# A GNN-and-mixture kernel for Trainium2: each group of TensorE products in the edge stages is announced by a drain behind it instead of by its last product

## The chip, the cores and the metric

The kernel runs on one core of one Trainium2 chip. The metric is device time of one execution in microseconds (us), the median of several runs without the profiler. Before the change it is 1890.13 us (three runs, 1889.97 to 1891.54).

## What is computed

Two layers over a graph of N = 3125 nodes with D = 256 features and E = 50000 edges (src, dst), the edges sorted by dst. Cut to what matters here:

```python
xn = layernorm(x)
# layer 0: attention over the edges (1 head, with self loops), then an LSTM cell; plus a linear-attention mixture
e     = leaky_relu(a_src[src] + a_dst[dst])
alpha = segment_softmax(e, dst)
agg   = segment_sum(alpha[:, None] * xp[src], dst)      # edge sums
x = x + cell(tanh(agg + bias)) + mixture0(xn)
x = x + top2_experts0(layernorm(x))
# layer 1: the same with 8 heads, no self loops, elu; plus a gated linear-attention mixture
x = x + elu(edge_sums(xn)) + mixture1(xn)
x = x + top2_experts1(layernorm(x))
```

dst is drawn as 3125 u^2 with u uniform, so the low-numbered nodes have by far the most edges.

## The kernel before, in words

Nodes are held in 25 tiles of 125 (`P`, `NT`). The sorted edges are cut into 98 blocks (`NBLK`) of 512, each of 4 parts of 128 (`BW`). A block that holds edges of several tiles is visited once for each, which makes 122 steps (`STEPS` = 98 + 25 - 1) in each layer. `edge_sums` (from L589, called once a layer) runs these steps on all engines at once, with the order of each engine's work written out by hand and semaphores between the engines:

- **POOL** (L671 to L680) issues 4 indirect gathers for each block, one for 128 edges, into a ring of `R` = 8 blocks (`rows`). From the ninth block on it waits for `freed`.
- **SP** (L657 to L668) waits for the landing of each block, tells `landed`, and passes `freed` on after the sums of an older block (`summed` in layer 0, `weighed` in layer 1).
- **DVE** (L836 to L855), in step i: reduces the scores (L832), marks which edge belongs to which node (`mark`, L812), makes the logits (L842 to L848), adds finished sums to `acc` (`add`, L805), does its part of the mixture, and weighs (`weigh`, L819 in layer 0, L822 in layer 1).
- **ACT** takes exponentials (L745 to L752) and copies the turned marks out of PSUM (`keep`, L762, after a wait for `turned` and `scored`).
- **TensorE** (PE), in step i: `sums(i - 4)` (L699: 4 f32 products, each of which the profile records as 2), `scores(i - 2)` (L707: 4 small bf16 products), the mixture's products `side.tensor(pe, i)`, then `turn(i)` (L718: 4 bf16 products). The last product of each group carries the semaphore increment that the waiting engines need (`summed`, `scored`, `turned`).

The mixtures `Mix0` and `Mix1` hang on the steps as `side`. In Mix0, a tile's keys (L1717) and its key-value sums (L1705, L1706) fall due in 5 of 9 steps from step 4 to about step 50; a tile's hidden layer (L1770) in each step from 71 to 95; its output (L1761) in each step from 89 to 113. In Mix1, keys (L1997) are due in steps 2 to 26, the context (L2015, then L2004 two steps later) in steps 31 to 59, and in every second step from 67 to about 117 an output product (L2047) and a query (L2052, L2056). The same form of announcement stands behind each of them.

The form that the change touches, and the loop that orders TensorE's work:

```python
ins = pe.matmul(sum_banks[p % 2][0:P, 0:W], left, right, start=(w == 0), stop=(w == BW - 1))
ins.then_inc(summed, 1)
...
for i in range(STEPS + 4):
    if valid(i - 4):
        sums(i - 4)
    if valid(i - 2):
        scores(i - 2)
    side.tensor(pe, i)
    if valid(i):
        turn(i)
```

Of the kernel before, what the change touches and what calls it, by code (L numbers as in the profile page):

```python
# [588 lines left out]
def edge_sums(nc, m, tag, H, side_of=None):  # L589
# [8 lines left out]
    with Stage(nc) as c:  # L598
# [58 lines left out]
        with nc.Block() as block:  # L657
# [24 lines left out]
            @block.tensor  # L682
            def _(pe):
                bounds.tensor(pe)
                slot_of = column(pe, SLOT, R - 1)

                def sums(p):
                    slot = slot_of(p) if H == 1 else None
                    pe.wait_ge(weighed, p + 1)
                    if H > 1:  # L690
                        pe.wait_ge(laid, p + 1)
                    if p >= 2:
                        pe.wait_ge(added, p - 1)
                    for w in range(BW):
                        if H == 1:
                            left, right = won[:, p % 2, w, :], rows[:, bass.ds(slot, 1), w, :].rearrange("p a x -> p (a x)")
                        else:
                            left, right = one[:, p % O, w, :], msg[:, p % 2, w, :]
                        ins = pe.matmul(sum_banks[p % 2][0:P, 0:W], left, right, start=(w == 0), stop=(w == BW - 1))  # L699
                    ins.then_inc(summed, 1)  # L700

                def scores(p):
                    pe.wait_ge(kept, p + 1)
                    if p >= 1:
                        pe.wait_ge(zchain, 4 * p - 3)
                    for w in range(BW):
                        ins = pe.matmul(scores_of[p % 2][:, w, :], oneT[:, p % 2, w * 128:(w + 1) * 128],  # L707
                                        stage[:, p % 4, :], start=True, stop=True)
                    ins.then_inc(scored, 1)

                def turn(p):
                    pe.wait_ge(marked, p + 1)
                    if p >= 1:
                        pe.wait_ge(kept, p)
                    for w in range(BW):
                        at = turn_bank[0:P, w * 128:(w + 1) * 128]
                        flags = one[:, p % O, w, :] if H == 1 else upper(one[:, p % O, w, :])
                        ins = pe.matmul(at, flags, ident[:, :], start=True, stop=True)  # L718
                    ins.then_inc(turned, 1)

                for i in range(STEPS + 4):
                    if valid(i - 4):
# [6 lines that stand above are left out]
# [905 lines left out]
class Mix0:  # L1634
# [59 lines left out]
    def tensor(self, pe, i):  # L1694
# [6 lines left out]
        for t in self.scale(i, 1):  # L1701
            s = t % self.KV
            pe.wait_ge(self.normed, t + 1)
            for k in range(KD):
                pe.matmul(total[:, k * W:(k + 1) * W], kv[0:P, s, k, 0:128], kv[0:P, s, 2 + k, :], start=False, stop=False, skip_group_check=True)  # L1705
                ins = pe.matmul(total[:, 2 * W + k:2 * W + k + 1], kv[0:P, s, 2 + k, 0:128], kv[0:P, s, 0, 128:129],  # L1706
                                start=False, stop=False, skip_group_check=True)
            ins.then_inc(self.summed, 1)
        for t in self.key(i):
            if t == 0:  # L1710
                pe.wait_ge(self.centred, 3)
            if t == 1:
                pe.wait_ge(self.qkept, 1)
            if t >= 2:
                pe.wait_ge(self.biased, t - 1)
            for k in range(KD):
                ins = pe.matmul(m.bank[4 + 3 * (t % 2)][0:P, :], m.xT[:, k, tile_cols(t)], m.wkv[:, k, :], start=(k == 0), stop=(k == KD - 1))  # L1717
            ins.then_inc(self.made, 1)
        if i == self.CLOSE:
            pe.matmul(total[:, 0:260], self.zeros[:, 0:128], self.zeros[:, :].unsqueeze(1).to_broadcast([P, 2, 130]),  # L1720
                      start=False, stop=True).then_inc(self.summed, 1)
        if i == self.CLOSE + 2:
            pe.wait_ge(self.widened, 1)
            for k in range(KD):
                ins = pe.matmul(m.bank[7][:, k * 128:(k + 1) * 128], self.wide[:, k, :], m.ident[:, :], start=True, stop=True)
            ins.then_inc(self.spread, 1)
        if i == 2:
            pe.wait_ge(self.split, 1)
            for k in range(KD):
                for b in range(KD):  # L1730
                    at = k * D + b * 128
                    ins = pe.transpose(m.bank[7][:, at:at + 128], m.wq[:, b, k * 128:(k + 1) * 128], m.ident[:, :])
            ins.then_inc(self.qturned, 1)
        if i == self.FOLD:
            pe.wait_ge(self.mixer, 1)
            for k in range(KD):
                ins = pe.transpose(m.bank[7][:, k * 128:(k + 1) * 128], m.kv[:, k, :], m.ident[:, :])
            ins.then_inc(self.flipped, 1)
        if i == self.FOLD + 2:
            pe.wait_ge(self.biased, NT)  # L1740
            pe.wait_ge(self.flat, 1)
            for k in range(KD):
                ins = pe.matmul(m.bank[4][:, k * D:(k + 1) * D], self.kvT[:, k, :], m.w1[:, k, :], start=True, stop=True)
            ins.then_inc(self.joined, 1)
        if i == self.FOLD + 4:
# [5 lines left out]
            for b in range(KD):  # L1751
                for k in range(KD):
                    ins = pe.matmul(total[:, b:b + 1], self.after[:, k, b * 128:(b + 1) * 128], m.bq[:, k:k + 1],
                                    start=(k == 0), stop=(k == KD - 1))
            ins.then_inc(self.mapped, 1)
        for t in self.output(i):
            pe.wait_ge(self.bent, 1 if t < self.BENT else 2)
            if t >= 2:
                pe.wait_ge(self.added, t - 1)
            for k in range(KD):  # L1760
                ins = pe.matmul(m.bank[4 + 3 * (t % 2)][0:P, 0:D], m.xT[:, k, tile_cols(t)], m.w2[:, k, :], start=(k == 0), stop=(k == KD - 1))  # L1761
            ins.then_inc(self.out, 1)
        for t in self.hide(i):
# [4 lines left out]
            for o in range(KD):  # L1768
                for k in range(KD):
                    ins = pe.matmul(total[:, o * 128:o * 128 + P], m.w1[:, k, o * 128:(o + 1) * 128], m.xT[:, k, tile_cols(t)],  # L1770
                                    start=(k == 0), stop=(k == KD - 1))
            ins.then_inc(self.hidden, 1)
        for b in range(KD):
            if i == self.GATES + 3 * b:
# [3 lines left out]
                for u in range(6):  # L1778
                    ins = pe.transpose(m.bank[5 + 2 * (u // 4)][:, (u % 4) * 128:(u % 4 + 1) * 128], m.gn[:, u, b * 128:(b + 1) * 128], m.ident[:, :])
                ins.then_inc(self.gturned, 1)  # L1780

# [140 lines left out]
class Mix1:  # L1922
# [46 lines left out]
    def tensor(self, pe, i):  # L1969
        m, total = self.m, self.m.bank[5]  # L1970
        blank = self.zeros[:, :].unsqueeze(1).to_broadcast([P, 4, 128])
        if i == 0:
# [3 lines left out]
            for g, tiles in enumerate(self.groups):  # L1976
                if g >= 2:
                    pe.wait_ge(self.gate_bent, g - 1)
                for t in tiles:
                    at = (t - tiles[0]) * P  # L1980
                    ins = pe.transpose(m.bank[4 + 3 * (g % 2)][0:D // 4, at:at + P], m.tail[:, t, HEADS:], m.ident[0:P, 0:P])
                ins.then_inc(self.zturned, 1)
        if i == 1:
            pe.wait_ge(self.gate_bent, len(self.groups))
            for k in range(KD):
                for b in range(KD):
                    at = k * D + b * 128
                    ins = pe.transpose(m.bank[7][:, at:at + 128], m.wqkv[:, b, k * 128:(k + 1) * 128], m.ident[:, :])
            ins.then_inc(self.qturned, 1)
        for t in self.key(i):  # L1990
# [4 lines left out]
            for o in range(KD):  # L1995
                for k in range(KD):
                    ins = pe.matmul(m.bank[4 + 3 * (t % 2)][:, o * 128:o * 128 + P], m.wqkv[:, k, D + o * 128:D + (o + 1) * 128],  # L1997
                                    m.xT[:, k, tile_cols(t)], start=(k == 0), stop=(k == KD - 1))
            ins.then_inc(self.made, 1)
        for t in self.context(i, 3):  # L2000
            s = t % 2
            pe.wait_ge(self.ekept, t + 1)
            for k in range(KD):
                ins = pe.matmul(total[:, k * D:(k + 1) * D], self.ek[:, s, k * 128:(k + 1) * 128], m.xs[:, t, :],  # L2004
                                start=False, stop=False, skip_group_check=True)
            ins.then_inc(self.summed, 1)
        for t in self.context(i, 1):
# [6 lines left out]
            for k in range(KD):  # L2014
                ins = pe.transpose(m.bank[4 + 3 * (t % 2)][0:P, k * 128:(k + 1) * 128], self.ekT[:, s, k, :], m.ident[:, :])  # L2015
            ins.then_inc(self.turned, 1)
        if i == self.CLOSE:
            pe.matmul(total[:, :], self.zeros[:, :], blank, start=False, stop=True).then_inc(self.summed, 1)
        if i == self.FOLD:
            pe.wait_ge(self.levelled, 1)  # L2020
            for k in range(KD):
                for b in range(KD):
                    at = k * D + b * 128
                    ins = pe.transpose(m.bank[7][:, at:at + 128], self.sums[:, k, b * 128:(b + 1) * 128], m.ident[:, :])
            ins.then_inc(self.flipped, 1)
        if i == self.FOLD + 2:
            pe.wait_ge(self.ekept, NT)
            pe.wait_ge(self.flat, 1)
            for k in range(KD):
                for b in range(KD):  # L2030
                    ins = pe.matmul(m.bank[4][:, k * 128:(k + 1) * 128], self.sumsT[:, k, b * 128:(b + 1) * 128],
                                    m.wqkv[:, b, 2 * D + k * 128:2 * D + (k + 1) * 128], start=(b == 0), stop=(b == KD - 1))
            ins.then_inc(self.crossed, 1)
        if i == self.FOLD + 4:
            pe.wait_ge(self.mixer, 1)
            for b in range(KD):
                for k in range(KD):
                    at = b * D + k * 128
                    ins = pe.matmul(m.bank[7][:, at:at + 128], self.wqT[:, k, b * 128:(b + 1) * 128], m.kv[:, k, :], start=True, stop=True)
            ins.then_inc(self.mapped, 1)  # L2040
        for t in self.output(i, 2):
# [4 lines left out]
            for k in range(KD):  # L2046
                ins = pe.matmul(m.bank[7][0:P, 0:D], self.goT[:, s, k, :], m.wproj[:, k, :], start=(k == 0), stop=(k == KD - 1))  # L2047
            ins.then_inc(self.out, 1)
        for t in self.output(i):
# [4 lines left out]
            for o in range(KD):  # L2054
                for k in range(KD):
                    ins = pe.matmul(total[:, o * 128:o * 128 + P], m.wqkv[:, k, o * 128:(o + 1) * 128], m.xT[:, k, tile_cols(t)],  # L2056
                                    start=(k == 0), stop=(k == KD - 1))
            ins.then_inc(self.queried, 1)

# [397 lines left out]
```

## Time and profile before

| | us |
|---|---|
| median of the runs without the profiler | 1890.13 |
| span of the profiled execution, first to last instruction | 2276.6 |
| TensorE busy in it | 1646.4 (72%) |
| VectorE (DVE) busy | 1163.6 (51%) |
| GpSimd (POOL) busy | 1009.6 (44%) |
| ScalarE (ACT) busy | 656.1 (29%) |
| steps of layer 0's edge stage, from the first turn to the last add | 77.4 to 745.0 |
| steps of layer 1's edge stage | 1201.7 to 1933.2 |

The profile is of one execution, and its span is 386.5 us longer than the median of the runs: here the two may not be taken for each other. In a row of the timeline stand the start, the length, the engine, the line, the operation with what it writes and reads, and the count; in brackets the idle time of the engine before it and what ended that. PEld is TensorE's weight load, which overlaps its products (PE). An engine's name with a q behind it is its sequencer. The ends of TensorE's products are modelled.

### The profile page before, as it was taken

How to read it: one execution, taken by the hardware profiler on the slowest of the kernel's cores; microseconds unless marked ns; L12 is line 12 of the kernel's file. 1: busy time of each engine (PE TensorE's matmuls, PEld its weight loads, DVE VectorE, ACT ScalarE, POOL GpSimd, SP SyncE). 2: the span in 40 equal slices, each digit the busy share in tenths (PEclk: the TensorE clock that was granted, in tenths of full speed). 3: DMA queues.
4: the chain of work that ended last, by engine and by line, in shares of the span. 5: the costliest groups of instructions: out<-in, count | busy, mean ns of one | idle time of the engine just before them, and what ended most of it. 6: DMA issues, size and time to landing. Idle time of an engine off the chain costs nothing. (4 is left out here: it accounts for less than half of the span.)

```text
span 2276.6 us, 34460 instructions
## 1 busy us (share of the span) xinstructions
PE 1646.4 (72%) x9468; PEld 1342.0 (59%) x9468; DVE 1163.6 (51%) x3309; ACT 656.1 (29%) x2160; POOL 1009.6 (44%) x1093
## 2 busy tenths in 40 slices
PE   5177776677778978999463665777577777689991
PEld 4045555556656557999343554555455556689991
DVE  7256566555456664222452555556566657841223
ACT  4222121122322554333152222332222212643330
POOL 4556555656543002555124545555454541325550
PEclk9588888889889989999786777888787989599996
DMA  7323222333222016666532222222222220267666
GB/s 167 98 71 84 80 75 75 87 82 87 78 70 58 1 63 224 211 213 210 135 112 72 80 74 77 74 80 75 70 77 68 72 72 20 93 199 213 215 202 178
DMA packets 148002, 244.24 MB, mean 107 GB/s; under 512 B 53369, under 2 KB 83368, under 8 KB 147558
## 3 DMA queue, kind: packets, MB, share of 16 engines
q0 software_dynamic: 48384, 134.19, 21.1%
q1 hardware_dynamic: 97306, 106.27, 15.7%
q10 hardware_dynamic: 2124, 1.54, 0.3%
q8 instruction: 85, 1.39, 0.2%
q14 instruction: 103, 0.84, 0.1%
HBM read 210.48 MB, written 31.21 MB: 106 GB/s over the span
## 5 line engine op out<-in xcount | busy, mean ns | idle before, releaser
L679 POOL DMA_INDIRECT es_rows<-table,eall x784 | 745.7, 951 | 719.3 <-SPq L668 418.6
L699 PE MATMUL bank<-es_msg,es_one 128*125 128x264 f32 x976 | 305.3, 466 | 123.5 <-DVE es_msg L822 104.1
L699 PE MATMUL bank<-es_rows,es_won 128*125 x976 | 289.8, 448 | 116.8 <-DVE es_won L819 84.8
L762 ACT ACTIVATE es_oneT<-bank 125x512 bf16<-125x512 f32 x244 | 145.1, 595 | 755.9 <-remote 488.5
L699 PEld LDWEIGHTS bank<-es_msg,es_one 128*125 128x125 f32 x976 | 209.0, 225 | 175.2 <-DVE es_msg L822 113.9
L699 PEld LDWEIGHTS bank<-es_rows,es_won 128*125 128x125 f32 x976 | 202.4, 218 | 159.2 <-issue 125.3
L842 DVE TENSOR_TENSOR es_z<-es_rows,es_near 128x4 f32<-128x4 f32 (+1 forms) x244 | 43.1, 177 | 359.3 <-ACTq L774 265.2
L1237 PE MATMUL bank<-ffn_xbT,ffn_w 128*128 128x128 f32 x1792 | 220.8, 277 | 0.0
L1290 ACT ACTIVATE xT<-bank,ffn_b1s 128x128 f32<-128x128 f32 x448 | 128.2, 369 | 303.2 <-PE bank L1237 292.6
L1396 DVE TENSOR_TENSOR xT<-bank,xT 128x256 f32<-128x256 f32 x112 | 47.6, 425 | 327.8 <-issue 190.1
L1247 PE MATMUL bank<-ffn_w,xT 128*128 x896 | 211.7, 379 | 0.0
L1237 PEld LDWEIGHTS bank<-ffn_xbT,ffn_w 128*128 128x128 f32 x1792 | 211.6, 194 | 0.1
L1186 POOL DMA_INDIRECT yrows<-xT,ffn_dst_i x112 | 110.8, 990 | 184.4 <-DVE xT L1396 184.4
L718 PE MATMUL bank<-es_ident,es_one 128*125 128x128 bf16 x976 | 108.2, 238 | 102.0 <-issue 54.0
L1247 PEld LDWEIGHTS bank<-ffn_w,xT 128*128 128x128 f32 x896 | 161.8, 190 | 17.6 <-issue 0.2
L718 PEld LDWEIGHTS bank<-es_ident,es_one 128*125 128x125 bf16 x976 | 93.5, 151 | 125.7 <-issue 122.4
L832 DVE TENSOR_REDUCE es_near<-bank 128x8 f32<-128x24 f32 (+1 forms) x244 | 65.2, 267 | 196.5 <-remote 122.7
L812 DVE TENSOR_TENSOR es_one<-nodes,bank 128x500 bf16 (+1 forms) x244 | 163.3, 669 | 3.6 <-issue 3.3
L1181 POOL DMA_INDIRECT ffn_xb<-xrows,ffn_src_i x112 | 108.8, 972 | 111.4 <-DVE ffn_dst_i L1375 77.2
L822 DVE TENSOR_TENSOR es_msg<-es_rows,bank 128x1024 f32<-128x1024 f32 x122 | 148.7, 1219 | 5.6 <-ACT bank L749 3.7
L707 PEld LDWEIGHTS bank<-es_stage,es_oneT 125*128 125x128 bf16 x976 | 64.3, 103 | 104.0 <-issue 72.5
L805 DVE TENSOR_TENSOR acc<-acc,bank 125x258 f32 (+1 forms) x244 | 104.2, 427 | 8.8 <-PE bank L699 3.8
(445 smaller groups left out, 2408.8 us busy)
## 6 DMA issues: line engine op xcount, KB each, us to landing
ffn_w<-in_L_ffn_W SPq DMA_DIRECT2D x112, 512.0 KB
es_rows<-table,eall POOLq DMA_INDIRECT x784
ffn_w<-yrows SPq DMA_DIRECT2D x20, 560.0 KB
ffn_w<-in_L_ffn_W SPq DMA_DIRECT2D x2, 4096.0 KB
xrows<-acc SPq DMA_DIRECT2D x10, 560.0 KB
table<-acc SPq DMA_DIRECT2D x5, 577.5 KB
table<-acc SPq DMA_DIRECT2D x5, 564.4 KB
out_x<-xs SPq DMA_DIRECT2D x5, 560.0 KB
```

The costliest lines, as they stand in the source:

```text
L679: pool.indirect_dma_start(rows[:, q % R, w, :], None, m.table[H], bass.IndirectOffsetOnAxis(ap=m.eall[:, at:at + 1], axis=0)).then_inc(gat ...
L699: ins = pe.matmul(sum_banks[p % 2][0:P, 0:W], left, right, start=(w == 0), stop=(w == BW - 1))
L718: ins = pe.matmul(at, flags, ident[:, :], start=True, stop=True)
L762: a.activation(oneT[:, p % 2, :], turn_bank[0:P, :], ACT.Copy).then_inc(kept, 1)
L805: v.tensor_tensor(acc, acc, sum_banks[p % 2][0:P, 0:W], ALU.add).then_inc(added, 1)
L812: v.tensor_tensor(one[:, p % O, :, :], nodes, own, ALU.is_equal).then_inc(marked, 1)
L822: v.tensor_tensor(msg[:, p % 2, :, 0:D].rearrange("p w (h x) -> p w h x", h=H), rows_of(p, 0, D).rearrange("p w (h x) -> p w h x", h=H), w ...
L1181: pool.indirect_dma_start(xb[:, j % SX, :], None, m.xrows, bass.IndirectOffsetOnAxis(ap=src_i[:, j:j + 1], axis=0)).then_inc(x_in[j % SX], 16)
L1186: pool.indirect_dma_start(m.yrows, bass.IndirectOffsetOnAxis(ap=dst_i[:, j:j + 1], axis=0), y[:, j % SY, :], None).then_inc(y_out[j % SY], 16)
L1237: ins = pe.matmul(hidden_banks[s][:, h * 128:(h + 1) * 128], w1[:, j % SW, k, h * 128:(h + 1) * 128], xbT[:, s, k, :], start=(k == 0), sto ...
L1247: ins = pe.matmul(out_banks[s][:, 0:D], hT[:, s, h, :], w2[:, bass.ds(e, 1), h, :].rearrange("p a d -> p (a d)"), start=(h == 0), stop=(h ...
L1290: ins = a.activation(hT[:, s, h, :], hidden_banks[s][:, h * 128:(h + 1) * 128], ACT.Gelu, bias=b1s[:, j % SW, h:h + 1])
```

## The change

In `edge_sums`, `Mix0.tensor` and `Mix1.tensor` every `ins.then_inc(semaphore, 1)` on the last product of a group becomes `pe.drain().then_inc(semaphore, 1)`: one more instruction on TensorE's queue behind the group, which carries the increment. No product, wait, tile or order changes. The diff, cut to its kinds:

```diff
@@ edge_sums, sums / scores / turn
-                    ins.then_inc(summed, 1)
+                    pe.drain().then_inc(summed, 1)
...
-                    ins.then_inc(scored, 1)
+                    pe.drain().then_inc(scored, 1)
...
-                    ins.then_inc(turned, 1)
+                    pe.drain().then_inc(turned, 1)
@@ Mix0.tensor
-            ins.then_inc(self.summed, 1)
+            pe.drain().then_inc(self.summed, 1)
...
-            ins.then_inc(self.made, 1)
+            pe.drain().then_inc(self.made, 1)
...
-            ins.then_inc(self.out, 1)
+            pe.drain().then_inc(self.out, 1)
...
-            ins.then_inc(self.hidden, 1)
+            pe.drain().then_inc(self.hidden, 1)
@@ Mix1.tensor
-            ins.then_inc(self.made, 1)
+            pe.drain().then_inc(self.made, 1)
...
-            ins.then_inc(self.summed, 1)
+            pe.drain().then_inc(self.summed, 1)
...
-            ins.then_inc(self.turned, 1)
+            pe.drain().then_inc(self.turned, 1)
...
-            ins.then_inc(self.out, 1)
+            pe.drain().then_inc(self.out, 1)
...
-            ins.then_inc(self.queried, 1)
+            pe.drain().then_inc(self.queried, 1)
```

Left out are the same edits of the groups that run once or a few times: in Mix0 `spread`, `qturned`, `flipped`, `joined`, `mapped` (once each) and `gturned` (twice); in Mix1 `zturned` (7 times), `qturned`, `flipped`, `crossed` and `mapped` (once each). The lone products that open and close an accumulation keep their own increment.

## Rows read from the trace of the kernel before

**Rows 1.** The page: span, busy time of each engine, TensorE's clock by slices
```profile
span 2276.6 us, 34460 instructions
PE 1646.4 (72%) x9468; PEld 1342.0 (59%) x9468; DVE 1163.6 (51%) x3309; ACT 656.1 (29%) x2160; POOL 1009.6 (44%) x1093
PEclk9588888889889989999786777888787989599996
```

**Rows 2.** The waits: who waited for whom, us in total, times, longest
```profile
ACT es_oneT L762 <- remote: 488.5, 81, 18.4
POOL es_rows L679 <- SPq L668: 418.6, 109, 14.7
...
POOL es_rows L679 <- issue: 211.4, 672, 1.4
...
DVE es_near L832 <- remote: 122.7, 43, 7.7
```

**Rows 3.** Timeline, layer 0: two announced groups and those who wait for them
```profile
404.00 0.24 PE L707 MATMUL bank<-es_stage,es_oneT 125*128 125x6 bf16 x4
...
404.99 0.42 PE L718 MATMUL bank<-es_ident,es_one 128*125 128x128 bf16 x4
...
409.94 0.18 DVE L832 TENSOR_REDUCE es_near<-bank 128x8 f32<-128x24 f32 x1 [3.71 <-remote]
410.09 0.60 ACT L762 ACTIVATE es_oneT<-bank 125x512 bf16<-125x512 f32 x1 [4.55 <-remote]
410.09 0.68 DVE L812 TENSOR_TENSOR es_one<-nodes,bank 128x500 bf16 x1
...
410.83 0.43 PE L718 MATMUL bank<-es_ident,es_one 128*125 128x128 bf16 x4 [0.32 <-DVE es_one L812]
```

**Rows 4.** The page's group of the gathers: busy, mean ns, idle before
```profile
L679 POOL DMA_INDIRECT es_rows<-table,eall x784 | 745.7, 951 | 719.3 <-SPq L668 418.6
```

**Rows 5.** Windows of the two edge stages: busy us of each engine, clock, DMA
```profile
77.40:745.00 667.60, 468.77 (x2597) 362.76 (x2595) 370.37 (x1163) 151.13 (x448) 365.96 (x385) 0.84 0.28 77
1201.70:1933.20 731.50, 495.82 (x2729) 392.94 (x2728) 423.97 (x1065) 181.12 (x694) 352.68 (x372) 0.82 0.26 70
```

**Rows 6.** Timeline of PE, layer 0: one full step, back to back
```profile
604.80 0.39 PE L718 MATMUL bank<-es_ident,es_one 128*125 128x128 bf16 x4
605.03 1.96 PE L699 MATMUL bank<-es_rows,es_won 128*125 x8
606.83 0.24 PE L707 MATMUL bank<-es_stage,es_oneT 125*128 125x6 bf16 x4
606.93 1.11 PE L1761 MATMUL bank<-w_w,xT 128*125 128x256 f32 x4
607.88 1.05 PE L1770 MATMUL bank<-xT,w_w 128*128 128x125 f32 x8
608.76 0.39 PE L718 MATMUL bank<-es_ident,es_one 128*125 128x128 bf16 x4
```

**Rows 7.** The drains on PE's sequencer at block ends, and products before one
```profile
L657 PEldq DRAIN  x2: 1647/1860/2073, 742.8 to 1930.6; - x2
...
741.72 2.71 PE L699 MATMUL bank<-es_rows,es_won 128*125 x10
...
L83 PEldq DRAIN  x7: 8/13/13, 66.5 to 2275.9; - x7
...
L83 PEldq EVENT_SEMAPHORE  x7: 51/51/51, 67.0 to 2276.5; - x7
```

**Rows 8.** Key and key-value products of Mix0: a group line, one step's edges
```profile
L1717 PE MATMUL bank<-w_kv,xT 128*125 128x512 f32 x100 | 52.3, 648 | 0.0
...
298.26 0.24 PE L707 MATMUL bank<-es_stage,es_oneT 125*128 125x6 bf16 x4
298.37 0.47 PE L1705 MATMUL bank<-mix_kv 125*128 125x129 f32 x2
...
299.26 0.42 PE L718 MATMUL bank<-es_ident,es_one 128*125 128x128 bf16 x4
```

**Rows 9.** Timeline of PE, layer 1: a context step, then an output step
```profile
1509.28 0.26 PE L707 MATMUL bank<-es_stage,es_oneT 125*128 125x48 bf16 x4
...
1512.62 0.27 PE L707 MATMUL bank<-es_stage,es_oneT 125*128 125x48 bf16 x4
...
1761.69 1.11 PE L2047 MATMUL bank<-w_proj,mix_slots 128*125 128x256 f32 x4
...
1764.36 0.40 PE L718 MATMUL bank<-es_ident,es_one 128*125 128x128 bf16 x4
```

**Rows 10.** Timeline of DVE, layer 1, two output steps: first and last rows
```profile
1817.34 0.36 DVE L832 TENSOR_REDUCE es_near<-bank 128x64 f32<-128x192 f32 x1 [4.27 <-remote]
...
1821.53 0.35 DVE L832 TENSOR_REDUCE es_near<-bank 128x64 f32<-128x192 f32 x1
...
1823.61 1.22 DVE L822 TENSOR_TENSOR es_msg<-es_rows,bank 128x1024 f32<-128x1024 f32 x1
```

More of the change, by code:

```diff
@@ L1725, in tensor @@
                 ins = pe.matmul(m.bank[7][:, k * 128:(k + 1) * 128], self.wide[:, k, :], m.ident[:, :], start=True, stop=True)
-            ins.then_inc(self.spread, 1)
+            pe.drain().then_inc(self.spread, 1)
         if i == 2:
@@ L1732, in tensor @@
                     ins = pe.transpose(m.bank[7][:, at:at + 128], m.wq[:, b, k * 128:(k + 1) * 128], m.ident[:, :])
-            ins.then_inc(self.qturned, 1)
+            pe.drain().then_inc(self.qturned, 1)
         if i == self.FOLD:
@@ L1737, in tensor @@
                 ins = pe.transpose(m.bank[7][:, k * 128:(k + 1) * 128], m.kv[:, k, :], m.ident[:, :])
-            ins.then_inc(self.flipped, 1)
+            pe.drain().then_inc(self.flipped, 1)
         if i == self.FOLD + 2:
@@ L1743, in tensor @@
                 ins = pe.matmul(m.bank[4][:, k * D:(k + 1) * D], self.kvT[:, k, :], m.w1[:, k, :], start=True, stop=True)
-            ins.then_inc(self.joined, 1)
+            pe.drain().then_inc(self.joined, 1)
         if i == self.FOLD + 4:
@@ L1754, in tensor @@
                                     start=(k == 0), stop=(k == KD - 1))
-            ins.then_inc(self.mapped, 1)
+            pe.drain().then_inc(self.mapped, 1)
         for t in self.output(i):
@@ L1779, in tensor @@
                     ins = pe.transpose(m.bank[5 + 2 * (u // 4)][:, (u % 4) * 128:(u % 4 + 1) * 128], m.gn[:, u, b * 128:(b + 1) * 128], m.ident[:, :])
-                ins.then_inc(self.gturned, 1)
+                pe.drain().then_inc(self.gturned, 1)
     def scalar(self, a, i):
@@ L1981, in tensor @@
                     ins = pe.transpose(m.bank[4 + 3 * (g % 2)][0:D // 4, at:at + P], m.tail[:, t, HEADS:], m.ident[0:P, 0:P])
-                ins.then_inc(self.zturned, 1)
+                pe.drain().then_inc(self.zturned, 1)
         if i == 1:
@@ L1988, in tensor @@
                     ins = pe.transpose(m.bank[7][:, at:at + 128], m.wqkv[:, b, k * 128:(k + 1) * 128], m.ident[:, :])
-            ins.then_inc(self.qturned, 1)
+            pe.drain().then_inc(self.qturned, 1)
         for t in self.key(i):
@@ L2024, in tensor @@
                     ins = pe.transpose(m.bank[7][:, at:at + 128], self.sums[:, k, b * 128:(b + 1) * 128], m.ident[:, :])
-            ins.then_inc(self.flipped, 1)
+            pe.drain().then_inc(self.flipped, 1)
         if i == self.FOLD + 2:
@@ L2032, in tensor @@
                                     m.wqkv[:, b, 2 * D + k * 128:2 * D + (k + 1) * 128], start=(b == 0), stop=(b == KD - 1))
-            ins.then_inc(self.crossed, 1)
+            pe.drain().then_inc(self.crossed, 1)
         if i == self.FOLD + 4:
@@ L2039, in tensor @@
                     ins = pe.matmul(m.bank[7][:, at:at + 128], self.wqT[:, k, b * 128:(b + 1) * 128], m.kv[:, k, :], start=True, stop=True)
-            ins.then_inc(self.mapped, 1)
+            pe.drain().then_inc(self.mapped, 1)
         for t in self.output(i, 2):
```

## The prediction

> **What bounds the kernel now.** I begin with the page, because the span and the median disagree: the profiled execution lasts 2276.6 us [rows 1], the runs 1890.13, so 386.5 us of what the trace shows is not in the measured time. The view of the waits tells where they probably sit. ACT's copy of the turned marks waits 488.5 us for a "remote" releaser, DVE's reduction of the scores 122.7, and POOL's gathers wait 418.6 us for SP to free a block [rows 2]. The timeline shows such a wait from near. The group L707 ends at 404.24 and the group L718 at 405.41; DVE, which waits for the first, starts at 409.94, and ACT, which waits for the second, at 410.09: the signals came 5.70 and 4.68 us after the products' ends, with both consumers idle [rows 3]. This is what a drain in place of the last product's increment seems to be aimed at.
>
> The question is whether the measured runs have this lateness at all. Take POOL's 418.6 us of waiting out of the span and 1858.0 remain, 32.1 under the median. So in the measured runs POOL can hardly wait: they look like runs in which gathers are issued without a stop. A gather takes 951 ns [rows 4] and the issue gap before the next 211.4 / 672 = 0.31 us [rows 2], so a block of four costs 4 x 1.265 = 5.06 us, and 98 blocks 496 us a layer. I read the late signals as something that the profiled execution adds. TensorE is not far behind POOL: its products fill 468.8 and 495.8 us of the two edge stages [rows 5], at a mean granted clock of 0.84 and 0.82, so partly at 1.2 GHz.
>
> By the Trainium skill (Runtime: NRT & Kernel Launch, the preamble and postamble breakdown) a profile's total stands some 6 us above the reported execution time whatever the kernel. By that rule the lateness would be in the runs too; the 386.5 us here speak against it.
>
> **The change part by part.** It adds one drain behind every group: 3 x 122 in each edge stage; in Mix0 25 each for keys, key-value sums, hidden layer and output, and 7 others; in Mix1 25 each for keys, both context groups, output and query, and 11 others. That is 473 and 502 drains. It removes only an increment that costs no instruction. Nothing moves on any other queue, and no DMA is issued earlier or later by the program; what changes is when TensorE goes on, and behind each drain stands everything that TensorE has left to do.
>
> *The price of one drain.* No drain stands between groups now. Those at the ends of program blocks show what one does: at L657 it takes 1647 ns, from 742.8, while the products before it end at 744.43, so it holds the queue until some 0.05 us after the last end; with nothing in flight it takes 13 ns [rows 7]. A group that starts now while the one before is still leaving the array will have to wait for that. The overlap lost is a group's own length less the distance to the next start: L718 0.39 - 0.23 = 0.16, L699 1.96 - 1.80 = 0.16, L707 0.24 - 0.10 = 0.14 [rows 6]. Behind the drain the next group's semaphore wait takes 0.05 on the sequencer [rows 7], today passed while products run, and the first product starts 0.06 after its release: DVE's mark ends at 410.77, L718 starts at 410.83 [rows 3]. Together 0.15 + 0.05 + 0.05 + 0.06 = 0.31 us. Upper end: a group with three such waits, 0.41. Lower end: 0.05, where TensorE was going to wait anyway, or below nothing if a drain's signal came earlier than the product's does; I take 0.31, since the rows nearest to the case are back-to-back steps.
>
> By the Trainium skill (PSUM — Partial Sum Buffer, Engine vs sequencer instructions) an increment on the product itself fires when the product completes, while a drain waits for the whole engine to go idle. By that rule there is no late signal to cure and the sum below stands; rows 3 contradict its first half in the profiled execution, rows 7 agree with the second.
>
> *What lies on the path.* A step gives POOL time to hide drains. After b blocks the walk is at step b + 25 (b/97.7)^2, because the edges crowd in the low tiles; one block's 5.06 us then spans 1 + 0.0052 b steps. That pace is some 4.6 us a step early and 3.4 at the end. TensorE's bare step, back to back, is 0.23 + 1.80 + 0.10 = 2.13 in layer 0 [rows 6], 2.17 in layer 1 by the same differences.
>
> Layer 0. Steps 4 to 50: keys 52.3 / 25 = 2.09 less an overlap of 0.16, key-value sums 299.26 - 298.37 = 0.89 [rows 8], due in 25 of 46 steps, so 1.53 a step; with 4.1 drains 2.13 + 1.53 + 1.27 = 4.93 against 4.55. The 17 us over are won back in steps 50 to 71, which carry no products of the mixture (3.06 against 3.95): nothing. Steps 71 to 89, hidden layer: 2.13 + 0.92 + 4 x 0.31 = 4.29 against 3.73, 18 x 0.56 = 10. Steps 89 to 96, hidden layer and output: 3.96 from one L718 to the next [rows 6] + 5 x 0.31 = 5.51 against 3.60, 7 x 1.91 = 13. Steps 96 to 113, output: 2.13 + 0.95 + 1.24 = 4.32 against 3.48, 18 x 0.84 = 15. Sum 38.
>
> Layer 1. Context, steps 31 to 59: 1512.62 - 1509.28 = 3.34 [rows 9] + 5 x 0.31 = 4.89 against 4.18, 25 x 0.71 = 18, of which 4 are won back before step 67. Steps 67 to 117: every second step adds 1764.36 - 1761.69 = 2.67 [rows 9], so on average 3.50 + 4 x 0.31 = 4.74. Today DVE sets this pace rather than POOL: its two steps take 4.19, and 3.30 without the mixture's part [rows 10], 3.75 on average. 50 x 0.99 = 50. Sum 64.
>
> Together +102 us: **1890 + 102 = 1992 us**. The sum is made from durations of the profiled execution but against the median, since the span's surplus is what I hold to be absent from the runs. At 0.20 us a drain the same stretches give 19 + 27 = +46 (1936), at 0.41 about 76 + 100 = +176 (2066).
>
> **The rivals.**
>
> *The drains are hidden* (1890). POOL's pace would have to cover them everywhere. For it: the light steps have 0.9 us to spare. Against it: TensorE's 470 to 500 busy us stand against 496 us of gathers, and steps 89 to 96 leave no room. It decides if a drain costs under some 0.10 us.
>
> *The late signals are real and the drain cures them: faster.* Place: `turned` and `scored` in the edge stages; TensorE's queue would post a drain's increment at once, where the product's is held back. For it: 611 us of remote waits [rows 2]. Against it: the runs have room for only the 32.1 us that POOL could still be waiting, from which drains in the crowded steps take a part. Taking a third off gives 1870, and 1858 if nothing is paid. It decides from a price under 0.10 us together with signals late in the runs.
>
> *The drain waits out the lateness.* If a drain cannot end before a held-back completion is acknowledged, TensorE stands still with it. At 0.5 us for each of 975 drains that is +490, most of it exposed: 2300.
>
> **How the numbers follow.** Forecast, stretches of TensorE that outgrow the gathers' pace: 0.64. Hidden: 0.14. Faster by the cure: 0.16. Waiting out the lateness: 0.06. So slower 0.70, same 0.14, faster 0.16, where 0.2% (3.8 us) is about what a measurement of this kernel tells from no change. The range runs from 1865, which takes in most of the cure, over the price's ends (1936, 2066) to 2085; beyond it lie the last rival and the outer part of the first case. The forecast's own range is 1936 to 2066.
>
> **What would show it.** In the changed kernel's profile: some 975 more drains on PE's sequencer, most of 0.2 us or more (they begin while products run); L699 after L718 starting about 0.5 us after L718's start instead of 0.23; hidden-layer and output steps of layer 0 above 4.2 us; POOL waiting for SP mainly in the late steps. The step on lateness is wrong if the measured time falls, and the price is wrong if the time rises by less than 46 or more than 176 us. If remote waits vanish from the profile and its span shrinks while the measured time grows, both halves of the argument hold.

## The result and the profile after

The changed kernel takes 2122.99 us in the median (2110.83 to 2126.85) against 1890.84 before: **12.1% slower**, a ratio of 1.1209 with a 95% interval of 1.1176 to 1.1243, +232 us. The forecast was slower, 1992 us; the measured time lies 38 us above the range's upper end.

The page of the changed kernel, the lines that answer to [rows 1]:

```profile
span 2125.1 us, 35435 instructions
PE 1673.6 (79%) x9468; PEld 1274.6 (60%) x9468; DVE 1170.6 (55%) x3309; ACT 656.6 (31%) x2160; POOL 1009.6 (48%) x1093
...
PEclk9698997699989998999988899999999998699995
```

This span agrees with the timed runs, where that of the first profile of the kernel before was 386 us over them. The waits of the changed kernel, to be set against [rows 2]:

```profile
ACT es_oneT L762 <- PEq L719: 702.4, 233, 9.3
...
DVE es_z L842 <- ACTq L774: 326.0, 165, 6.4
...
POOL es_rows L679 <- SPq L668: 263.5, 85, 11.3
...
DVE es_near L832 <- PEq L709: 71.7, 82, 3.9
```

"remote" is gone: what ACT waits for now is TensorE's sequencer at L719, the drain behind the turns. That by itself says nothing about what the drains brought, as the control below shows. The timeline of PE in the changed kernel, layer 0, a step with key-value sums, against [rows 6] and [rows 8]:

```profile
400.25 0.24 PE L707 MATMUL bank<-es_stage,es_oneT 125*128 125x6 bf16 x4 [0.23 <-issue]
400.72 0.41 PE L718 MATMUL bank<-es_ident,es_one 128*125 128x128 bf16 x4 [0.23 <-issue]
401.46 2.00 PE L699 MATMUL bank<-es_rows,es_won 128*125 x8 [0.33 <-issue]
403.69 0.24 PE L707 MATMUL bank<-es_stage,es_oneT 125*128 125x6 bf16 x4 [0.23 <-issue]
404.01 0.48 PE L1705 MATMUL bank<-mix_kv 125*128 125x129 f32 x2
...
405.29 0.41 PE L718 MATMUL bank<-es_ident,es_one 128*125 128x128 bf16 x4 [0.23 <-issue]
```

Each group now stands alone. The weight loads stop too: before L707 PEld is idle for 157.0 us with only its sequencer to wait for, 5.5 in the second profile of the kernel before (the control below). From one start to the next, scores to turn take 0.47 us where scores took 0.10, turn to sums 0.74 instead of 0.23, sums to scores 2.23 instead of 1.80, key-value sums to turn 1.28 instead of 0.89. The bare step, 3.44 us from the scores at 400.25 to those at 403.69, was 2.13: three drains cost 1.31, **0.44 us each**. The brackets show the part that the forecast had too small: 0.23 us (0.33 before the sums of layer 0) in which TensorE is empty and waits for nothing but its own sequencer. In layer 1 no 0.33 appears:

```profile
1698.19 0.42 PE L718 MATMUL bank<-es_ident,es_one 128*125 128x128 bf16 x4 [0.23 <-issue]
1698.85 2.02 PE L699 MATMUL bank<-es_msg,es_one 128*125 128x264 f32 x8 [0.23 <-issue]
1701.09 0.26 PE L707 MATMUL bank<-es_stage,es_oneT 125*128 125x48 bf16 x4 [0.23 <-issue]
1701.58 0.42 PE L718 MATMUL bank<-es_ident,es_one 128*125 128x128 bf16 x4 [0.23 <-issue]
```

From turn to turn that is 3.39 us against 2.17, 0.41 us a drain.

The drains in the trace, all three kinds of the edge sums (ns, min/median/max):

```profile
L700 PEldq DRAIN  x244: 1468/2017/3577, 88.6 to 1780.5; - x122
...
L709 PEldq DRAIN  x244: 115/244/322, 78.3 to 1776.9; - x122
...
L719 PEldq DRAIN  x244: 253/418/1632, 75.1 to 1771.3; - x122
```

They begin while the products run and end just behind them, as [rows 7] had it.

### The profile page after: what moved, and what is told of

Read it like the earlier page. It is cut to its first block and busy times, and to the rows that moved or that the text cites. A ratio compares the mean times of both kernels' runs of the same rounds, so it can differ in the third digit from the quotient of the medians.

```text
span 2125.1 us, 35435 instructions
## 1 busy us (share of the span) xinstructions
PE 1673.6 (79%) x9468; PEld 1274.6 (60%) x9468; DVE 1170.6 (55%) x3309; ACT 656.6 (31%) x2160; POOL 1009.6 (48%) x1093
## 5 line engine op out<-in xcount | busy, mean ns | idle before, releaser
L679 POOL DMA_INDIRECT es_rows<-table,eall x784 | 746.0, 951 | 564.1 <-SPq L668 263.5
L699 PE MATMUL bank<-es_rows,es_won 128*125 x976 | 279.8, 435 | 72.9 <-issue 40.0
L699 PE MATMUL bank<-es_msg,es_one 128*125 128x264 f32 x976 | 251.0, 401 | 43.1 <-DVE es_msg L822 24.0
L699 PEld LDWEIGHTS bank<-es_rows,es_won 128*125 128x125 f32 x976 | 193.8, 209 | 120.2 <-issue 90.0
L699 PEld LDWEIGHTS bank<-es_msg,es_one 128*125 128x125 f32 x976 | 175.5, 190 | 83.9 <-DVE es_msg L822 29.8
L718 PE MATMUL bank<-es_ident,es_one 128*125 128x128 bf16 x976 | 105.6, 233 | 56.9 <-issue 53.5
L718 PEld LDWEIGHTS bank<-es_ident,es_one 128*125 128x125 bf16 x976 | 78.9, 142 | 114.2 <-issue 88.7
L707 PEld LDWEIGHTS bank<-es_stage,es_oneT 125*128 125x128 bf16 x976 | 43.7, 96 | 157.0 <-issue 157.0
L707 PE MATMUL bank<-es_stage,es_oneT 125*128 125x6 bf16 (+1 forms) x976 | 61.2, 175 | 56.9 <-issue 56.2
```

The costliest lines, as they stand in the source:

```text
L679: pool.indirect_dma_start(rows[:, q % R, w, :], None, m.table[H], bass.IndirectOffsetOnAxis(ap=m.eall[:, at:at + 1], axis=0)).then_inc(gat ...
```

## The experiments

| kernel | us, median | ratio to the kernel before | 95% interval |
|---|---|---|---|
| control (unchanged) | 1889.76 | 1.0013 | 1.0000 to 1.0026 |
| changed kernel | 2122.99 | 1.1209 | 1.1176 to 1.1243 |
| kept | 2116.64 | 1.1236 | 1.1190 to 1.1282 |
| edges_only | 2029.99 | 1.0755 | 1.0728 to 1.0782 |
| mix_only | 1949.16 | 1.0320 | 1.0300 to 1.0341 |
| turn_only | 1912.70 | 1.0122 | 1.0105 to 1.0139 |
| scores_only | 1919.69 | 1.0160 | 1.0145 to 1.0174 |
| sums_only | 1935.18 | 1.0241 | 1.0225 to 1.0256 |
| double | 2228.81 | 1.1746 | 1.1673 to 1.1819 |
| half_before | 1882.91 | 0.9969 | 0.9959 to 0.9979 |
| half_after | 2116.69 | 1.1213 | 1.1190 to 1.1237 |
| early_ready | 1858.32 | 0.9821 | 0.9800 to 0.9841 |
| early_half | 1786.98 | 0.9448 | 0.9432 to 0.9464 |
| early_drains | 2072.34 | 1.0943 | 1.0922 to 1.0965 |
| early_half_drains | 2065.61 | 1.0928 | 1.0907 to 1.0950 |

A ratio is taken against runs of the kernel before that were measured beside the kernel in question (medians of 1888.8 to 1892.8 us), and is not exactly the quotient of two medians. The four kernels with `half` in their names leave out half of the edges' rows, so they tell of pace alone.

### control: were the late signals ever in the timed runs?

The kernel before, without an edit.

> The kernel before, unchanged, for a second profile and for the span and granted clock of its timed runs. If late signals come with the profile alone: the timed runs stay at 1890 us, and the profile, if it is long again (about 2270 us), shows remote waits again. If the first profile was one disturbed execution: this profile's span is near 1889 us and the remote waits are gone. Clock: if the changed kernel loses time because TensorE stands more often at 1.2 GHz, the runs of this one have a granted clock clearly above 0.92; if not, 0.92 or less.

Its page and waits:

```profile
span 1885.9 us, 34460 instructions
...
PE 1521.3 (81%) x9468; PEld 1263.3 (67%) x9468; DVE 1156.6 (61%) x3309; ACT 657.7 (35%) x2160; POOL 1009.2 (54%) x1093
```

```profile
ACT es_oneT L762 <- PE bank L718: 354.8, 210, 7.9
...
DVE es_z L842 <- ACTq L774: 156.5, 127, 5.0
...
POOL es_rows L679 <- SPq L668: 20.3, 12, 4.4
```

The second reading holds: the span is that of the runs, and no wait is "remote". The timeline shows how soon a last product's increment is seen:

```profile
542.44 0.39 PE L718 MATMUL bank<-es_ident,es_one 128*125 128x128 bf16 x4
...
542.87 0.60 ACT L762 ACTIVATE es_oneT<-bank 125x512 bf16<-125x512 f32 x1 [1.70 <-PE bank L718]
```

ACT starts 0.04 us after the products' end at 542.83. In the changed kernel the drain's increment takes 0.02 longer: the turn at 400.72 ends at 401.13, and ACT starts at 401.19. The lateness that the change seems aimed at belonged to one profiled execution. The granted clock over the whole execution is 0.922, as in the changed kernel (0.92): a lower mean clock is not where the time went, though by stage it moved, as the next rows show.

The control gives the true edge stages of the kernel before; here they stand, and behind them those of the changed kernel (busy us of PE, PEld, DVE, ACT, POOL, then clock, DMA share, GB/s):

```profile
78.20:587.70 509.50, 423.71 (x2597) 334.84 (x2595) 365.95 (x1163) 151.61 (x448) 365.26 (x385) 0.93 0.37 101
1034.30:1543.40 509.10, 417.80 (x2729) 343.30 (x2729) 421.67 (x1065) 183.08 (x694) 359.26 (x378) 0.97 0.37 102
```

```profile
76.10:737.80 661.70, 516.73 (x2597) 349.82 (x2595) 376.79 (x1163) 151.62 (x448) 367.34 (x385) 0.89 0.29 78
1185.10:1783.10 598.00, 479.70 (x2728) 341.36 (x2728) 424.69 (x1065) 181.66 (x694) 356.70 (x378) 0.99 0.32 87
```

Layer 0 loses 661.7 - 509.5 = 152.2 us, layer 1 88.9, together 241, against 239.2 between the two spans: all of the loss lies in the edge stages.

### kept: the stop or the signal?

```diff
-                    pe.drain().then_inc(summed, 1)
+                    ins.then_inc(summed, 1)
+                    pe.drain()
```

(the same at all 23 places)

> The increments go back to the last products, and the drains stand behind the groups with no increment. If the time is lost because TensorE stops at each drain: as the changed kernel, 2100 to 2125 us, since the consumers' signals come only some 0.05 us earlier. If it is lost because the drains' signals reach the consumers later: near 1890 us. If late signals come with increments on products: the profile of this kernel shows remote waits again, and a span far over its timed runs.

It takes 2116.64 us, within 7 us of the changed kernel. The loss is TensorE's stop, not the way the consumers are told. No remote waits came back.

### edges_only and mix_only

Drains at L700, L709 and L719 alone, or at the other 20 places alone.

> Drains behind the three groups of the edge sums alone (732 of 975), the mixtures announce by their last product. Price on TensorE's path (0.44 us a drain as the changed kernel's trace shows it: bare step 3.44 instead of 2.13): layer 0 loses 47 us in the stretches where the step outgrows the gathers, layer 1 62 us, so about 2000 us; a bare step of 3.44 us. If the cost came from the mixtures' long groups instead: under 1930 us.

> Drains behind the mixtures' groups alone (243 of 975). Price on TensorE's path: nearly all of it is covered by the gathers' pace, 10 to 30 us over before, so 1900 to 1920 us. If each drain costs time wherever it stands (232 us / 975 = 0.24 us each): 1890 + 58 = 1948 us.

The drains of the edge sums alone cost 140 us over before (1889.48 here), 30 more than expected. Those of the mixtures cost 60, where their hiding under the gathers' pace would have left 10 to 30; this is the 0.24 us a drain of the second theory. The cover that the gathers' pace was to give was in doubt from here on.

### turn_only, scores_only, sums_only

> The drain behind the turns alone (244). Behind a turn stand the sums of the next step, which in the kernel before often wait for VectorE's weights (168 us in 106 waits in its second profile). If a drain is free where TensorE would wait anyway: about 25 us over before, 1915 us. If every drain costs the same (140 us / 732 = 0.19 us each): 1890 + 47 = 1937 us.

> The drain behind the scores alone (244). Behind it TensorE has the mixture's products or the turn ready, so nothing covers it on TensorE; the changed kernel's trace gives 0.47 us from the scores' start to the next group's instead of 0.10, so 0.37 us each. Price on the path, as far as the gathers' pace does not cover it: 30 to 50 us, 1920 to 1940 us. If the three groups' drains are alike: as turn_only within 10 us.

> The drain behind the sums alone (244): 2.23 us from the sums' start to the scores' instead of 1.80, 0.43 us each. Price on the path: 40 to 60 us, 1930 to 1950 us, the most of the three. If the three are alike: as turn_only within 10 us. The three single ones together give less than edges_only's 140 us if a first drain is partly covered by the gathers' pace, and 140 us if each drain costs its own.

24, 31 and 46 us over the kernel before (1888.82 here): 0.10, 0.13 and 0.19 us for each of 244 drains. The order is the expected one. Turns are probably cheapest because the sums behind them often wait for VectorE anyway, and then have no overlap to lose; in the control, layer 1:

```profile
1453.85 2.04 PE L699 MATMUL bank<-es_msg,es_one 128*125 128x264 f32 x8 [1.56 <-DVE es_msg L822]
```

Together they make 101 us where edges_only has 140. That the first drain in a step falls into such waits and the next ones find them used up can be only part of it: TensorE's waits for VectorE's `es_won` and `es_msg`, 168.2 us in the control, shrink by 35, 36 and 42 us in the three single kernels and by 99 in edges_only, so 14 of the 39 us come from there. The rest was not traced.

### double: what is the price made of?

```diff
+                    pe.drain()
                     pe.drain().then_inc(summed, 1)
```

> A second drain right behind each of the 975, which finds TensorE empty (13 ns in the block ends' rows). If a drain's price is the overlap lost while the array empties: the second is nearly free, at most 975 x 0.02 = 20 us over the changed kernel, 2120 to 2140 us. If a good part of the price is the sequencer's time for one more instruction (0.1 us lie between a drain's end and the next instruction in the changed kernel's trace): 0.1 us each, mostly on the path, 2190 to 2220 us.

It takes 2228.81 us, 106 more than the changed kernel for 975 more drains, which would be 0.11 us each: the second reading, 9 us beyond its upper end. Yet the second drain itself takes 13 ns (first and second drain behind the turns, ns):

```profile
L721 PEldq DRAIN  x244: 259/423/1630, 76.3 to 1867.3; - x122
...
L722 PEldq DRAIN  x244: 13/13/141, 78.0 to 1867.8; - x122
```

The timeline tells the price of the second drain without the rest of the execution (the lines have moved by up to two):

```profile
406.17 0.24 PE L708 MATMUL bank<-es_stage,es_oneT 125*128 125x6 bf16 x4 [0.31 <-issue]
406.72 0.41 PE L720 MATMUL bank<-es_ident,es_one 128*125 128x128 bf16 x4 [0.31 <-issue]
407.54 2.00 PE L699 MATMUL bank<-es_rows,es_won 128*125 x8 [0.41 <-issue]
409.85 0.24 PE L708 MATMUL bank<-es_stage,es_oneT 125*128 125x6 bf16 x4 [0.31 <-issue]
```

Each of the three distances, 0.55, 0.82 and 2.31, is 0.08 us longer than in the changed kernel. So about 0.08 us passes on TensorE's sequencer around a drain that has nothing to wait for; the record of the drain does not hold it. For 975 drains that is 78 us. The other 28 go with a lower granted clock (0.895 to 0.919 in the runs of `double`, 0.92 to 0.93 in those of the changed kernel): the run at 0.919 took 2199.97 us, 77 over the changed kernel.

### half_before and half_after: do the gathers set the pace?

```diff
-                    for w in range(BW):
+                    for w in range(2):
                         at = (q * BW + w) * 2
```

(and the other half of the ring set to zero once a layer)

> The kernel before with two of the four gathers of each block; the other half of the ring is set to zero once a layer, so half of the edges' rows are left out and POOL's work in the edge stages is halved. If the gathers' pace bounds the kernel before: the edge stages shrink from 509 us each toward TensorE's own steps (some 420 to 440), so 1720 to 1760 us. If TensorE or VectorE bounds it: over 1860 us.

> The changed kernel with the same half of the gathers. If TensorE's drained steps set its pace: POOL's relief gives little, 2000 to 2070 us, and the distance to half_before is near the whole price of the drains with nothing to cover it, 975 x 0.3 to 0.4 = 260 to 360 us. If the gathers still bound it: the same fall as before's.

Halving POOL's gathers brings 6 us before and 6 us after. The forecast's bound falls. For half_after both readings missed: it gave less than the 2000 to 2070 us expected, and stands 234 us over half_before where 260 to 360 were expected. In half_before:

```profile
POOL es_rows L682 <- SPq L670: 537.7, 179, 9.5
...
DVE es_z L845 <- ACTq L777: 150.7, 116, 5.0
```

POOL now waits 537.7 us for blocks to come free, and VectorE's logits still wait 150.7 us for ACT's sequencer at L777. That line (L774 in the kernel before) is `ready`, which ACT passes on when a block has landed. It is not late because of the landing: ACT comes to it only behind `keep(i)`, which waits for TensorE's turn of the step. So there is a loop: turn, ACT, `ready`, logits, weights, the sums of a later step.

### early_ready, early_half, early_drains, early_half_drains: the loop taken apart

```diff
                     if valid(i - 3):
                         expose(i - 3)
-                    if valid(i):
-                        keep(i)
                     if valid(i - 2):
                         a.wait_ge(landed, block_of(i - 2) + 1)
                         a.sem_inc(ready, 1)
+                    if valid(i):
+                        keep(i)
```

> The kernel before, with ACT's pass-on of ready (two steps back) moved ahead of its wait for the step's turn. VectorE waits 156 us for that signal in the kernel before. If the loop through ready and the gathers' pace both bind at nearly the same length: only what POOL still waits can be won, 20 to 30 us, 1860 to 1872 us. If the loop alone binds: 1780 us or less. If neither: 1889 us.

> half_before with the same move: half of the gathers and of the edges' rows left out, ready passed on early. If the loop through ready is what held half_before at 1883 us: the edge stages fall toward TensorE's own busy time (some 420 us of 509 each), 1720 to 1780 us. If TensorE's or VectorE's work itself holds it: over 1860 us.

> The changed kernel, drains and all, with ready passed on early. If the drains cost so much because they lengthen TensorE's part of that loop: a good part comes back, 1990 to 2060 us. If TensorE alone, one drained step after another, sets the pace: within 20 us of 2123.

> early_half with all 975 drains (half of the gathers and of the edges' rows left out). If TensorE alone, drain behind drain, sets the pace of the drained kernel: as early_drains, 2050 to 2075 us, so 265 to 290 us over early_half, or 0.27 to 0.30 us for each drain with nothing in the gathers to cover it. If the gathers still held early_drains: under 2000 us.

early_ready takes 1858.32 us, a ratio of 0.9821 (0.9800 to 0.9841), 34 us under before and 2 us below the first reading's stretch: close to it, so the loop and the gathers bind at nearly the same length. Its waits of POOL for the ring's blocks and of VectorE for `ready`:

```profile
DVE es_z L842 <- ACTq L772: 70.3, 55, 3.6
...
POOL es_rows L679 <- SPq L668: 0.3, 1, 0.3
```

POOL waits once for SP, 0.3 us in all: now the gathers do set the pace. With both taken away, early_half falls to 1786.98 us, 96 under half_before, and 7 us above the stretch expected; its wait for `ready` is nearly gone:

```profile
POOL es_rows L682 <- SPq L670: 446.2, 176, 9.7
...
DVE es_z L845 <- ACTq L775: 7.8, 14, 1.6
```

With the drains in, the move brings 51 us (early_drains 2072.34, between the two readings), less than the 63 at least that was expected, and it brings 34 without them: some 16 of the 232 went round the loop. And early_half_drains, with gathers and loop relieved, stays at 2065.61, inside the first reading's stretch: TensorE's drained queue sets that pace, 279 us over early_half, 0.29 us a drain. The windows of the two edge stages, early_half first:

```profile
79.30:523.10 443.80, 406.57 (x2597) 325.30 (x2595) 366.94 (x1163) 146.35 (x448) 180.21 (x190) 0.95 0.22 58
971.00:1443.60 472.60, 408.21 (x2729) 337.82 (x2728) 417.38 (x1065) 179.00 (x694) 172.54 (x183) 0.99 0.20 54
```

```profile
79.10:692.90 613.80, 483.55 (x2597) 330.91 (x2595) 376.87 (x1163) 143.07 (x448) 179.90 (x190) 0.95 0.15 42
1146.30:1730.30 584.00, 479.32 (x2728) 342.68 (x2728) 421.90 (x1065) 175.79 (x694) 171.49 (x181) 0.99 0.16 43
```

## Why the prediction was right or wrong

**The late signals: right.** They were held to be absent from the timed runs, since POOL's waits of 418.6 us [rows 2] taken out of the span left 1858. The control shows POOL waiting 20.3 us, where the working left 32.1, and no late signal. The rivals built on them, the cure and the drain that waits out the lateness, fall with that. The sign that was to show both halves (remote waits gone, a shorter span, a longer time) came out too, but the control, which has no remote waits and no drains, shows that it could not tell. The rule of the Trainium skill (Runtime: NRT & Kernel Launch, the preamble and postamble breakdown), a profile's total some 6 us above the reported time, is not what the control shows: its span, from first to last instruction, is 1885.9 us, 3.9 below the median of 1889.76. That span and runs agree within a few us holds there; the first profile was the exception.

**The price of a drain: the step that failed first.** 0.31 us was put together from the overlap lost (0.15), the end of the drain (0.05), the next wait (0.05) and the restart (0.06). The overlap was right, about 0.16 us in [rows 6]. What lies between the products' end and the next start was put at 0.16 and measured 0.23, and 0.33 before the sums of layer 0. Some 0.08 us of that is the drain's own passage through the sequencer, which the timeline of `double` shows and which no row of before showed; the 0.15 that is left is close to the 0.16 of the forecast. The upper end, 0.41, is what the back-to-back step of layer 1 measured, and lay below the 0.44 of layer 0. By the prediction's own scale (46 at 0.20 us, 102 at 0.31, 176 at 0.41) 0.41 to 0.44 would have given 176 to close to 200, still short of 232.

**The cover: the step that failed second.** "That pace" of the gathers was to hide the drains of the early steps and of the light ones. Step lengths, read from the starts of L718 in the control and in the changed kernel:

| stretch | forecast loss, us | measured |
|---|---|---|
| layer 0, steps 4 to 50 | 17 | 45.9 |
| layer 0, steps 50 to 71 | -17 | 28.2 |
| layer 0, steps 71 to 89 | 10 | 24.7 |
| layer 0, steps 89 to 96 | 13 | 13.5 |
| layer 0, steps 96 to 114 | 15 | 29.7 |
| layer 1, steps 4 to 31 | none given | 22.9 |
| layer 1, steps 31 to 59 | 18 | 29.3 |
| layer 1, steps 71 to 114 | 43 (of 50) | 30.2 |

Steps 89 to 96 came out right by two errors: set against the gathers' 3.60 us, where TensorE's own step of 3.96 was the bound (28.0 / 7 = 4.00 in the control), with a price too low. Where the forecast saw slack it was wrong: nothing was won back after step 50. Steps 50 to 71 do carry products of the mixture: the key-value sums run from step 17 to step 60 (those at 404.01 in the changed kernel are of step 58), and five single groups follow up to step 69. In this stretch the granted clock also fell, from 0.94 in the control to 0.81. As to the slack itself, half_before shows why it was not there: the gathers were one of two bounds that lay close together, and halving them left the steps of layer 0 as long as they were (steps 4 to 50 took 222.8 us instead of 221.5; only in layer 1's steps 31 to 59 did it help, 103.6 instead of 114.0). POOL's own waits say the same: of 263.5 us in the changed kernel 60.7 (between 94 and 361 us of its span) fall into steps 4 to 50 already, and some 136, about half, into the steps from 71 on, where the forecast saw them mainly. What hid drains instead was TensorE's own waiting for VectorE. Its waits in the control, then in the changed kernel:

```profile
PE bank L699 <- DVE es_msg L822: 89.9, 65, 4.7
PE bank L699 <- DVE es_won L819: 78.3, 41, 5.1
```

```profile
PE bank L699 <- issue: 59.1, 186, 1.1
PE bank L707 <- issue: 56.2, 241, 0.4
PE bank L718 <- issue: 53.5, 229, 0.4
PE bank L699 <- DVE es_won L819: 32.9, 19, 4.3
...
PE bank L699 <- DVE es_msg L822: 24.0, 39, 3.7
```

111 us of waiting (168.2 less 56.9) took in drains. Against it stand 168.8 us in which TensorE is empty before the groups of the edge sums, and 155 us more of busy time in the two stages (996.4 against 841.5), near the 975 x 0.16 of overlap lost. So, as an estimate, the drains cost over 320 us before anything hid them, where 0.31 us each would be 302, and 111 were hidden, where the forecast of 102 had hidden 200: the cover was the larger of the two errors. In layer 1's output steps the forecast was too high, because it set the drained steps against VectorE's work of 3.75 us, and the control's steps took 79.8 / 18 = 4.43 there (steps 71 to 89).

**What made up the rest.** Without the gathers and the loop, early_half_drains less early_half, a drain costs 0.29 us; in the kernel as it was 232 / 975 = 0.24. The 0.29 is still net of hiding: TensorE's waits for `es_won` and `es_msg` fall from 94.2 us in early_half to 19.7. In layer 0 the granted clock also fell from 0.93 to 0.89 in the edge stage, while it rose from 0.97 to 0.99 in layer 1. At the two levels of 1.2 and 2.4 GHz that is 0.22 x 661.7 = 146 us at the lower one instead of 0.14 x 509.5 = 71. It can hold part of the 63 us by which layer 0 lost more than layer 1. It need not hold all: early_half_drains lost 170.0 us in layer 0 and 111.4 in layer 1 against early_half, 59 more in layer 0, with the clock of each layer unchanged (0.95 and 0.99). There layer 1 had more waiting to give up: `es_msg` fell from 61.9 to 8.8 us, `es_won` in layer 0 from 32.3 to 10.9. What share the clock has in the changed kernel stays open.

## What to carry to other kernels

A drain on TensorE's queue stopped weight loads and products alike and cost 0.41 to 0.44 us in a back-to-back step, 0.29 on average with gathers and loop relieved; an increment on the last product adds no instruction to the queue and was seen 0.02 us sooner. Before a change is aimed at a wait of the profile, see whether the profile's span agrees with the timed runs, and if not, take a second profile. That an engine never waits does not make it the bound: halve its work and measure, and where two bounds lie close together relieve both before either is dismissed.

## What the hardware showed that was not expected

In one profiled execution of an unchanged kernel the increments of TensorE's products were seen many microseconds after the products' modelled ends (5.70 us in [rows 3]). Its edge stages were 158.1 and 222.4 us longer than in the control, which holds nearly all of the 386 us; another profile of the same kernel has none of it. What set it off was not found.

An empty drain is recorded with 13 ns and takes 0.08 us of the queue. Of the 0.44 us that a drain takes in a bare step, some 0.16 are products that would have overlapped; the larger part passes on the sequencer, with the array empty.
